# An attention and slot-mixing kernel: last group reordered, three batches mixed by split products

## The reference

```python
q, k, v = mlp(x, W1q, ...), mlp(x, W1k, ...), mlp(x, W1v, ...)      # gelu(x @ W1 + b1) @ W2 + b2
scores = einsum('bid,bjd->bij', q, k) / scale * tril                # no softmax: linear in k, v
x = layernorm(x + layernorm_w(einsum('bij,bjd->bid', scores, v)))   # "x1" in the kernel
xn = layernorm(x) * gamma + beta
logits = einsum('bnd,des->bnes', l2norm(xn) * scale, l2norm(mu))    # 16 experts x 16 slots = 256
dispatch, combine = softmax(logits, tokens), softmax(logits, slots)
slot_in = einsum('bnd,bnes->besd', xn, dispatch)
slot_out = gelu(slot_in @ w1 + b1) @ w2 + b2
out = layernorm(x + einsum('besd,bnes->bnd', slot_out, combine))    # "mixing"
```

## Time and profile before

| what | value |
|---|---|
| median of 3 runs | 590.03 us (589.85 to 590.4) |
| profiled execution, its own time | 590.34 us |
| its span | 588.6 us |
| instructions in it | 11698 |
| busy: PE, PEld, DVE, ACT, POOL | 97, 90, 83, 67, 67 % of the span |
| DMA | 47.04 MB, mean 80 GB/s |
| granted TensorE clock | 1.00 of full speed, until the last slice |

### The profile page before, as it was taken

One profiled execution on the slowest core, in us unless ns is written; L12 is line 12 of the kernel. 1 busy time (PEld: TensorE's weight loads), 2 busy tenths in 40 slices (PEclk: granted clock), 3 DMA queues, 4 the chain that ended last, 5 costly groups with the idle time before them and its releaser, 6 DMA issues. The chain is left out here.

```text
span 588.6 us, 11698 instructions
## 1 busy us (share of the span) xinstructions
PE 572.5 (97%) x3796; PEld 528.0 (90%) x3796; DVE 485.6 (83%) x1048; ACT 393.4 (67%) x855; POOL 393.9 (67%) x395
## 2 busy tenths in 40 slices
PE   9999999999999999999999999979999999999994
PEld 7889989999999999999998999968999999888883
DVE  6579889899898898888989989979988777557885
ACT  4765666676766667667677666567688777435765
POOL 0869779789797797787977978785646443104453
PEclk9999999999999999999999999999999999999998
DMA  8324134043141331422403403105555555923445
GB/s 234 81 73 108 22 87 99 12 107 43 65 107 18 89 71 41 102 33 74 107 13 94 86 23 74 26 11 98 84 72 72 73 73 73 147 33 108 143 144 179
DMA packets 163473, 47.04 MB, mean 80 GB/s; under 512 B 139470, under 2 KB 159340, under 8 KB 163436
## 3 DMA queue, kind: packets, MB, share of 16 engines
q1 hardware_dynamic: 163424, 46.57, 36.9%
q10 hardware_dynamic: 12, 0.00, 0.0%
HBM read 21.39 MB, written 8.39 MB: 51 GB/s over the span
## 5 line engine op out<-in xcount | busy, mean ns | idle before, releaser
L523 POOL TENSOR_TENSOR h_lo<-xn_all,h_hi 128x512 fp32r<-128x512 f32 x32 | 41.4, 1295 | 68.2 <-ACT xn_all L649 67.1
L647 ACT ACTIVATE h_hi<-bank,bias_col 128x512 fp32r<-128x512 f32 x96 | 66.4, 692 | 18.8 <-PE bank L793 17.1
L791 PE MATMUL bank<-xnT_hi,w_hi 128*128 128x512 f32 x188 | 76.2, 405 | 0.0
L792 PE MATMUL bank<-xnT_lo,w_hi 128*128 128x512 f32 x188 | 74.4, 396 | 0.0
L793 PE MATMUL bank<-xnT_hi,w_lo 128*128 128x512 f32 x188 | 74.2, 395 | 0.0
L682 ACT CAST state_hi<-bank 128x512 fp32r<-128x512 f32 x57 | 33.5, 588 | 50.1 <-PE bank L926 50.1
L1608 PE MATMUL bank<-xn_all,e_tok 128*128 128x257 f32 x256 | 65.1, 379 | 0.0
L1190 DVE TENSOR_TENSOR state_lo<-bank,state_hi 128x512 fp32r<-128x512 f32 x57 | 39.4, 691 | 29.0 <-ACT state_hi L682 29.0
L1686 PE MATMUL bank<-w_sb,ET_all 128*128 128x256 f32 x256 | 55.4, 379 | 0.0
L1686 PEld LDWEIGHTS bank<-w_sb,ET_all 128*128 128x128 f32 x256 | 48.6, 190 | 6.6
L1507 ACT ACTIVATE e_tok<-bank,shift,xinv 128x256 f32<-128x256 f32 x64 | 36.1, 565 | 27.3 <-PE bank L1598 20.5
(11 more groups left out here) (202 smaller groups left out, 2081.6 us busy)
## 6 DMA issues: line engine op xcount, KB each, us to landing
x_all<-in_L_attn_x SPq DMA_DIRECT2D x16, 512.0 KB, 3.9
kT<-k_turn SPq DMA_DIRECT2D x128, 64.0 KB, 2.5
ET_all<-e_turn SPq DMA_DIRECT2D x64, 128.0 KB, 3.8
xn_all<-in_xT SPq DMA_DIRECT2D x15, 512.0 KB, 4.7
out<-xn_all SPq DMA_DIRECT2D x15, 512.0 KB, 3.0
w_sb<-in_L_ffn_w SPq DMA_DIRECT2D x2, 512.0 KB, 5.3
xn_all<-in_L_ffn_w SPq DMA_DIRECT2D x2, 512.0 KB, 6.6
xn_all<-in_xT SPq DMA_DIRECT2D x2, 256.0 KB, 3.5
```

The lines of the kernel that those rows point to most:

```text
L523: pool.tensor_tensor(h_lo[:, V_SLOT, m, :], hv[:, m, :], h_hi[:, V_SLOT, m, :].bitcast(F32), ALU.subtract).then_inc(hv_split, 1)
L647: nc.scalar.activation(h_hi[:, h_slot(j, n), m, :], ps, ACT.Gelu, bias=bias(n, m))
L791: nc.tensor.matmul(ps, w[0], xs[0], start=start, stop=False, skip_group_check=shared)
L792: nc.tensor.matmul(ps, w[0], xs[1], start=False, stop=False, skip_group_check=shared)
```

## The change

1. **Last attention group.** The division of group 1's tokens goes from GpSimd (one operation) to ScalarE (four activations, one per tile), and their weighting goes behind the last split on GpSimd's list. On VectorE, the sums of v for three tiles now follow `bias_v`, and `add_out` of tiles 2 and 3 goes into `last_body`. ScalarE's list of the end is reordered. `tok_weighted` replaces the count that `weight_tokens` gave.
2. **Mixing of batches 1 to 3** (groups 4 to 15) by three f32r products in place of one f32 product. ScalarE rounds ET_all of each group into ET_hi (`round_e`, 128x1024), GpSimd subtracts it in place into ET_lo (`split_e`, 128x1024). Groups 4 to 12 are split during routing, groups 13 to 15 during groups 1 to 3 of mixing. ScalarE's copies of batches 1 to 3 are f32r, and VectorE forms so_lo (three subtractions of 128x512).
3. **Room for it.** ET_hi lies where x1_all lies, group by group. So SP spills x1 of groups 4 to 15 to DRAM during routing (512 KB each) and reloads it later into buffers that are free by then (`reload_x1`); the sums and the residual of these groups read x1_again and wait for the reload.
4. **Order of mixing.** The first sum of group k + 1 moves between the two statistics of group k. The last group is reordered; tile 0 is normalised by VectorE, and the store of tiles 0 and 1 is issued by ScalarE.

The core of the diff:

```diff
@@ -556,24 +562,18 @@
-        def divide_tokens(k, q):
...
-            pool.tensor_tensor(xn[q][:, :, 0:D], x1_all[:, GT * k:GT * k + GT, :],
-                               r2_all[:, GT * k:GT * k + GT].unsqueeze(2).to_broadcast([P, GT, D]),
-                               ALU.mult).then_inc(tok_divided, 1)
...
         def weight_tokens(q):
-            pool.wait_ge(tok_divided, 1)
+            pool.wait_ge(tok_divided, GT)
             pool.tensor_tensor(xn[q][:, :, 0:D], xn[q][:, :, 0:D],
                                g_rows[:, :].unsqueeze(1).to_broadcast([P, GT, D]), ALU.mult
-                               ).then_inc(tok_scaled, GT)
+                               ).then_inc(tok_weighted, 1)
...
                 split_vsum(a, 1)
+                invert_norms(pool, 0, 0, minus_half[:, :])
+                weight_tokens(1)
                 add_beta(pool, 1, 1)
@@ -597,14 +597,11 @@
                 add_ln_b(g)
-            if not more:
-                divide_tokens(1, 1)
-                weight_tokens(1)
             split_ktok(g, 0)
+            if attend:
+                invert_o(pool, a, 1)
             if not more:
                 split_v(g, 0)
-            if attend:
-                invert_o(pool, a, 1)
             split_ktok(g, 1)
@@ -680,6 +675,15 @@
             nc.scalar.copy(to[:, :, :], state_halves).then_inc(state_rounded, 1)
...
+        def divide_tokens(k, q, tiles):
+            act.wait_ge(x1_ready, GT * k + 3 * GT)
+            act.wait_ge(r2_ready, k + 3)
+            act.wait_ge(hv_split, 2 * GROUPS)
+            for t in tiles:
+                tile = GT * k + t
+                nc.scalar.activation(xn[q][:, t, 0:D], x1_all[:, tile, :], ACT.Copy,
+                                     scale=r2_all[:, tile:tile + 1]).then_inc(tok_divided, 1)
@@ -720,13 +724,13 @@
                 round_xnT(act, 0, 0)
-                apply_z(act, a - 2, ja % 2, (0,))
+                round_vsum(a, 1)
                 round_state(ba, i + 2, tail_hi[2])
                 round_masked(a)
-                round_vsum(a, 1)
-                apply_z(act, a - 2, ja % 2, (1, 2))
+                divide_tokens(1, 1, (3,))
+                apply_z(act, a - 2, ja % 2, (0, 1))
                 round_state(ba, i + 3, tail_hi[3])
-                apply_z(act, a - 2, ja % 2, (3,))
+                apply_z(act, a - 2, ja % 2, (2, 3))
                 nc.scalar.activation(warm[:, :], warm[:, :], ACT.Exp).then_inc(table_warm, 1)
@@ -770,7 +774,11 @@
             round_ktok(g)
+            if not more:
+                divide_tokens(1, 1, (0, 1))
             round_v(g, 0)
+            if not more:
+                divide_tokens(1, 1, (2,))
             round_v(g, 1)
@@ -1267,10 +1275,11 @@
                     sum_v(g, j, 0)
+                    sum_v(g, j, 1)
+                    sum_v(g, j, 2)
+                    return
                 add_out(dve, a, 2)
                 add_out(dve, a, 3)
-                if not more:
-                    return
                 z_summed(dve, a, 1)
@@ -1286,10 +1295,10 @@
             mask_scores(a)
-            sum_v(a, ja, 1)
-            sum_v(a, ja, 2)
+            add_out(dve, a - 1, 2)
             tail_state(2)
             split_masked(a)
+            add_out(dve, a - 1, 3)
             split_xnT(dve, 0, 0)
@@ -1419,21 +1452,47 @@
+        def spill_x1(g):
+            sp.wait_ge(tok_scaled, GT * g)
...
+            sp.dma_start(x1_spill[n], x1_all[:, GT * g:GT * g + GT, :]).then_inc(x1_spilled[n % 2], 16)
...
+        def reload_x1(g):
+            n = g - FIRST
+            if g < AGAIN:
+                sp.wait_ge(logits_done, TILES)
+                for i in range(2):
+                    sp.wait_ge(e_moved[i], 16 * FOUR * GROUPS // 2)
+                    sp.wait_ge(x1_spilled[i], 16 * (n // 2 + 1))
+            else:
+                sp.wait_ge(mixed, GT * (g - AGAIN) + GT)
+                sp.wait_ge(x1_spilled[n % 2], 16 * (n // 2 + 1))
+            if n > 1:
+                sp.wait_ge(x1_reloaded[n % 2], 16 * (n // 2))
+            sp.dma_start(x1_again[g], x1_spill[n]).then_inc(x1_reloaded[n % 2], 16)
...
         for g in range(GROUPS):
+            if g + GB - 1 in SPLIT_GROUPS:
+                spill_x1(g + GB - 1)
             exchange_e(g)
...
                                  w2.rearrange("(r two) h d -> two h r d", two=2)[w]).then_inc(w2_loaded, 16)
+        for g in range(FIRST, AGAIN):
+            reload_x1(g)
         for k in range(LAST):
+            if k + AGAIN in SPLIT_GROUPS:
+                reload_x1(k + AGAIN)
             sp.wait_ge(y_normed, GT * k + GT)
             sp.dma_start(out_t[:, GT * k:GT * k + GT, :], y[k % GB][:, :, 0:D]).then_inc(stored[k % GB], 16)
...
         for q in range(GB):
@@ -1445,6 +1504,12 @@
             pool.memset(xn[q][:, :, D:D + 1], 1.0).then_inc(ones_set, 1)
...
+        def split_e(g):
+            pool.wait_ge(e_rounded, g - FIRST + 1)
+            exact = ET_all[:, g, :, :]
+            pool.tensor_tensor(ET_lo[:, g, :, :], exact, ET_hi[:, g, :, :].bitcast(F32), ALU.subtract
+                               ).then_inc(e_split, 1)
@@ -1455,6 +1520,8 @@
                     add_beta(pool, GB * b + q + 3, (q + 3) % GB)
+                if GB * b + q - 2 in SPLIT_GROUPS and not (last and q == GB - 1):
+                    split_e(GB * b + q - 2)
                 if b == 0 and q == 2:
@@ -1471,13 +1538,18 @@
         pool.wait_ge(e_turned, TILES + GT)
+        pool.wait_ge(e_split, GROUPS - GB - FIRST + 1)
         for w in range(2):
...
             yk = y[k % GB][:, SUMMED, 0:D]
-            pool.tensor_tensor(yk, yk, x1_all[:, GT * k + SUMMED, :], ALU.add).then_inc(y_added, 1)
+            x1 = x1_all[:, GT * k + SUMMED, :]
+            if k in SPLIT_GROUPS:
+                pool.wait_ge(x1_reloaded[(k - FIRST) % 2], 16 * ((k - FIRST) // 2 + 1))
+                x1 = x1_again[k][:, SUMMED, :]
+            pool.tensor_tensor(yk, yk, x1, ALU.add).then_inc(y_added, 1)
@@ -1494,6 +1566,8 @@
             invert_deviation(k)
+            if 0 < k < GB:
+                split_e(GROUPS - GB + k)
         for pair in range(2):
@@ -1518,6 +1592,14 @@
                     norms(act, k, q, (2, 3))
+            if t % GT == GT - 1 and k - 3 in SPLIT_GROUPS and not (last and q == 0):
+                round_e(k - 3)
...
+        def round_e(g):
+            n = g - FIRST
+            act.wait_ge(e_moved[g % 2], 16 * FOUR * (g // 2 + 1))
+            act.wait_ge(x1_spilled[n % 2], 16 * (n // 2 + 1))
+            nc.scalar.copy(ET_hi[:, g, :, :], ET_all[:, g, :, :]).then_inc(e_rounded, 1)
@@ -1575,12 +1657,17 @@
                 norm_y(k - 1)
+            if 0 < k < GB:
+                round_e(GROUPS - GB + k)
         norm_y(LAST - 1)
         act.wait_ge(y_shift, LAST + 1)
-        for t in range(2):
-            yt = y[LAST % GB][:, t, 0:D]
-            nc.scalar.activation(yt, yt, ACT.Identity, scale=rs_y[:, LAST % 2, t:t + 1],
-                                 bias=nm_y[:, LAST % 2, t:t + 1]).then_inc(y_normed, 1)
...
+        act.dma_start(out_t[:, GT * LAST:GT * LAST + 2, :], y[LAST % GB][:, 0:2, 0:D]
+                      ).then_inc(stored[LAST % GB], 16)
@@ -1682,9 +1769,22 @@
                     pe.wait_ge(mix_scaled, k - 1)
+                if k < 2 and t >= 2 and (t, t - 2)[k] in SO_ORDER:
+                    pe.wait_ge(so_split, SO_ORDER.index((t, t - 2)[k]) + 1)
+                if k in SPLIT_GROUPS and t == 0:
+                    pe.wait_ge(so_split, len(SPLIT))
+                    pe.wait_ge(e_split, k - FIRST + 1)
+                ps = mix_ps[k % 2][t][:, 0:D]
                 for s in range(SB):
-                    last = nc.tensor.matmul(mix_ps[k % 2][t][:, 0:D], ET_all[:, k, GT * s + t, :],
-                                            so[:, k // GB, s, :], start=(s == 0), stop=(s == SB - 1))
+                    if k in SPLIT_GROUPS:
+                        hi, lo = ET_hi[:, k, GT * s + t, :], ET_lo[:, k, GT * s + t, :]
+                        out_hi, out_lo = so_hi[:, k // GB, s, :], so_lo[:, k // GB - SPLIT[0], s, :]
+                        nc.tensor.matmul(ps, hi, out_hi, start=(s == 0), stop=False)
+                        nc.tensor.matmul(ps, hi, out_lo, start=False, stop=False)
+                        last = nc.tensor.matmul(ps, lo, out_hi, start=False, stop=(s == SB - 1))
+                    else:
+                        last = nc.tensor.matmul(ps, ET_all[:, k, GT * s + t, :], so[:, k // GB, s, :],
+                                                start=(s == 0), stop=(s == SB - 1))
                 last.then_inc(mixed, 1)
@@ -1789,20 +1889,30 @@
+        for n in SO_ORDER:
+            dve.wait_ge(so_ready, n + 1)
+            nc.vector.tensor_tensor(so_lo[:, n - SPLIT[0], :, :],
+                                    so_ps[n][:, :].rearrange("p (s d) -> p s d", s=SB),
+                                    so_hi[:, n, :, :].bitcast(F32), ALU.subtract).then_inc(so_split, 1)
...
```

(67 more changed lines are left out.)

23 lines of the change are left out of this document (13 added, 10 removed).

## The result

The changed kernel takes **598.54 us** (median of 5 runs, 596.77 to 598.83), the kernel before 590.4 beside it: ratio 1.0131, 95% interval 1.0114 to 1.0148. It is slower, as predicted, but 6.5 us above the forecast and 0.9 above the top of the range. Its profiled execution took 597.48, with a span of 595.6: 7.0 more than before.

The account below looks back on a forecast made before the run. TensorE bounded routing and mixing before; VectorE was to bound mixing from group 4. Terms +0.2 (attention end), +5.1 (groups 1 to 3), -3.05 (groups 4 to 14), -0.4 (end) sum to +1.85: forecast 592.0 us, range 589.0 to 597.6.

Parts of the forecast that it names:

- the part on groups 4 to 14: Mixing, groups 4 to 14: VectorE becomes the bound at 3.15 us a group, ten periods at 0.30 less, -3.05 us.
- The loop's other terms: VectorE's mixing loop: 1.30 to the shift, 0.08, first statistics 0.62, sum 0.41, second statistics 0.74, together 3.15 us.
- the first rival: Mixing: GpSimd's residual goes ahead of VectorE's shift, loop 3.65, ten periods +1.95 instead of -3.05, total 597.4 us; chance 0.27.
- Groups 1 to 3: Mixing, groups 1 to 3: second statistics wait for GpSimd's residual behind a split, 5.14 instead of 3.455 a group, +5.1 us.
- The end of attention: Last attention group reordered: v_lo ready earlier, but VectorE waits on GpSimd's splits; +0.2 us, bounds -2.5 and +0.6.
- where it was said to: Attention end: the wait for v_lo goes and one for the second state, of some 3 us, takes its place.
- Routing: Added roundings, splits and spills during routing: cost 0, up to 1 us with the cover gone.
- The end: Last mixing group: one sum of 0.41 moved forward, tile 0's normalisation fits into a VectorE wait, -0.4 us.
- The range: Whole kernel: 589.0 to 597.6 us, leaving out TensorE's pace and the far tail of the shift-shut-out case.
- TensorE keeps the pace: Rival for mixing: power hidden or late splits free, groups run at 2.88, total 583 to 585 us; chance 0.09.

Follow-up runs that it names:

- The early splits: Changed kernel with the roundings and splits of groups 13 to 15 moved ahead of the mixing: 592.52 us, ratio 1.0027.
- the two edits together: Changed kernel with GpSimd's residual waiting for VectorE's shift and the splits of groups 13 to 15 ahead of the mixing: 588.57 us, ratio 0.9969.
- the first and third of the last versions: Changed kernel with splits 13-15 before mixing, first sum back, old attention end; first: residual waiting for shift, 586.75 us; third: shift behind first statistics, fourth-tile scaling earlier, 586.39 us.

## Why the prediction was right or wrong

**The failing step** is in the part on groups 4 to 14: "The shift itself is priced as in the row, 0.03 after the power." The row had no residual beside it. In the changed kernel GpSimd's residual begins 0.06 ahead of the shift and holds it to its end, so that the shift takes 0.59 instead of 0.16. The loop's other terms held: where the shift is free, the groups come 3.125 apart against 3.15. The shift at 0.59 moved the following statistics by 0.43, the other terms were 0.03 shorter: 0.40 a group, which over ten groups makes +1.00 of -3.05. Between the two traces the sum missed by 5.15 (+7.0 against +1.85), and 4.05 of it is this term.

This was the first rival's mechanism. It was given 0.27, although the prediction found on its side and no row against it. Its sum of 597.4 lies 0.1 from the profiled execution and 1.1 below the median, and that it comes so near is partly luck: its loop of 3.65 was 0.95 too dear over groups 4 to 14 and it took 0.36 too much for groups 1 to 3, while the terms that it shared with the forecast were too low by 0.39 in the end of attention, 0.12 in routing and 0.52 in the last stretch.

The Trainium skill, SBUF — State Buffer, section Who interferes with whom, says that the engine which issues first keeps the shared port pair for its whole instruction. The traces agree, down to a lead of 0.01 with a hold of 0.64, and add that the next instruction of the same engine does not keep the other out if a gap of 0.08 lies between.

**Groups 1 to 3** were right: +5.24 for +5.1, with splits of 2.36 to 2.42 (2.4 taken). The mechanism was right for two of the three splits; behind the second the shift is held instead of the statistics, at about the same cost. The early splits show that nothing else is behind it.

**The end of attention**: 0.59 measured, 0.5 to 1.2 over the traces, for the +0.2 taken; the upper bound was +0.6. TensorE waits where it was said to, on VectorE and on TensorE:

```profile
387.65 1.23 DVE L243 TENSOR_SCALAR n_low<-n 128x4 f32<-128x4 f32 x1
388.79 0.68 DVE L1198 TENSOR_TENSOR h_lo<-bank,h_hi 128x512 fp32r<-128x512 f32 x1
```
```profile
389.53 0.39 PE L934 MATMUL bank<-v_hi,ktok_hi 128*128 128x256 f32 x1 [2.88 <-DVE h_lo L1198]
```

The wait for v_lo is gone, and one of 2.88 for the second state stands in its place. The prediction's steps came to 398.1 for the end of the block, and the scalings do end at 398.14; it then took off 0.3 because its sum for the old order was late by that, and that is most of the miss. How the end comes about differs from trace to trace. Where the clock stays up, the scalings are held 1.84 by the addition of beta (1.1 before: 2.75 against the free 1.66). Where it falls behind the idle 2.88, as in the changed kernel's trace, the third state comes late. The prediction did not price the clock.

**Routing** cost nothing in this trace, as said, and no sum waits for a store or a reload in a loop of 3.09 or more; only at 2.72 do the stores matter. **The end**: the part up to the last normalisation gained 0.22 (-0.4 forecast), but the span then runs on for 4.09 where it was 3.75, so +0.12 in all; what makes that last part longer was not tried. **The range** failed by its top. It was cut at the first rival's value, with no room for the runs' own spread (596.77 to 598.83) or for the attention term beside it. The profiled execution, at 597.48, lies inside it; the median lies 1.06 higher, and no trace shows one of the slower executions of this kernel. In runs with the same end of attention the block takes up to 18.75, and routing up to 1.98 more where the clock falls; that this makes the spread here is not shown.

That TensorE keeps the pace was rightly given little for this kernel, where it has gaps from 546 on. With both hold-ups removed, groups 4 to 14 come 2.97 to 3.12 apart on VectorE where the shift is free, and TensorE is then busy without a gap from 526 to 573 (the two edits together, and the first and third of the last versions): VectorE's loop is still the longer one, but TensorE's 2.85 is close below it.

## What to carry to other kernels

When work moves, look at what starts beside each small operation on the engine that shares a port: a 128x4 operation can cost as much as the 128x1024 one it meets. If two such operations are released by the same event, order them with a wait so that the short one goes first, or put the long one where the other engine has work with one input in SBUF. And count how many operations hide a latency before taking one of them away: here three sums hid the power exactly, and two did not.

## What was not expected of the hardware

TensorE's clock after the same idle time differed from run to run. In the changed kernel the granted clock after the idle 2.88 was 0.56 (stretch; its length, TensorE's busy time, granted clock, DMA share, GB/s):

```profile
390.00:392.00 2.00, 2.00 (x13) 0.56 0.03 8
```

That is near the level of 1.2 GHz, and products came 0.21 apart instead of 0.12. Of the seven traces with this order and the same idle time, the clock fell in four and stayed at 1.00 in three. With the old end it also fell in two of five traces, after a wait of 2.4, and cost nothing there (17.57 and 17.55).

In the three traces where it held, TensorE idled again ahead of routing, for 2.14 to 2.16 (1.17 before). In one of them, where the residual waits for the shift, the clock stayed at 1.00 there too. In the other two it fell: routing up to ve_y of group 0 took 1.98 longer than in the changed kernel with the residual done twice, and 1.30 longer with the two edits together. From the latter:

```profile
400.00:402.00 2.00, 2.00 (x11) 0.50 1.22 254
```

Which idle stretch is followed by a fall stays open; no run here tells.
